# Half of the addition of four sum pairs a tile moved from VectorE to GpSimd, in a pairwise-interaction tower

## What is computed

```python
e = jnp.stack([tbl_0[ids[:, 0]], ..., tbl_31[ids[:, 31]]], axis=1)   # (1024, 32, 64)
p, q = e[:, ROW_IDX], e[:, COL_IDX]              # all pairs i < j: 496
z = jnp.einsum('bne,hne,bnh->bn', p, kernel, q)  # kernel (64, 496, 64)
h = jnp.concatenate([z, dense_ctx], axis=1)      # 496 + 16 = 512
h = jnp.maximum(h @ W_top1 + b_top1, 0.0)        # 512 -> 512
h = jnp.maximum(h @ W_top2 + b_top2, 0.0)        # 512 -> 256
y = h @ W_top3                                   # 256 -> 1
```

## Time and profile before

| | us |
|---|---|
| timed runs, median of 3 | 391.67 (391.31 to 391.91) |
| profiled execution, its span | 467.8 |
| TensorE matmuls busy | 402.3 |
| VectorE busy | 354.2 |
| ScalarE busy | 335.2 |
| GpSimd busy | 241.7 |

### The profile page before, as it was taken

One profiled execution on the slowest core, in us unless ns is written; L12 is line 12 of the kernel. 1 busy time (PEld: TensorE's weight loads), 2 busy tenths in 40 slices (PEclk: granted clock), 3 DMA queues, 4 the chain that ended last, 5 costly groups with the idle time before them and its releaser, 6 DMA issues.

```text
span 467.8 us, 13484 instructions
## 1 busy us (share of the span) xinstructions
PE 402.3 (86%) x4800; PEld 298.7 (64%) x4800; DVE 354.2 (76%) x449; ACT 335.2 (72%) x2889; POOL 241.7 (52%) x260
## 2 busy tenths in 40 slices
PE   0537869598898989999999989999999989999997
PEld 0425645467766776677756776677757776668765
DVE  0226757577888978887888978887887978888982
ACT  1216656658689685969689685969689685969894
POOL 5555555545555556555555555555555555552000
PEclk9978789799999999999999999999999999999999
DMA  3564560101111011101111011101111111110000
GB/s 73 180 207 158 165 190 18 21 18 22 22 24 22 19 24 22 23 22 22 21 26 21 20 24 22 23 20 22 22 23 24 20 24 22 22 21 15 2 2 1
DMA packets 14563, 19.27 MB, mean 41 GB/s; under 512 B 7192, under 2 KB 7840, under 8 KB 14496
## 3 DMA queue, kind: packets, MB, share of 16 engines
q0 software_dynamic: 8192, 8.40, 9.1%
q1 hardware_dynamic: 6304, 10.00, 6.7%
HBM read 18.39 MB, written 0.00 MB: 39 GB/s over the span
## 4 chain that ended last, share of the span: by engine, by line
PE 61%; DVE 18%; issue 9%; another core or an unknown queue 6%; ACT 3%; POOL 1%; DMA 1%; DVEq 0%
PE u_ps L628 24%; PE u_ps L621 20%; DVE prod_s L537 9%; PE side_ps L642 9%; DVE prod_t L520 6%; ACT prod_s L432 3%; PE side_ps L677 2%; PE u_ps L604 2%; PE acc_ps L677 2%; DVE h L551 2%; POOL emb L383 1%; PE u_ps L708 1%; PE side_ps L701 1%; DVE emb_t L509 1%
## 5 line engine op out<-in xcount | busy, mean ns | idle before, releaser
L432 ACT ACTIVATE prod_s<-prod_s 128x64 f32<-128x64 f32 x1405 | 307.9, 304 | 76.2 <-DVE prod_s L537 66.2
L383 POOL DMA_INDIRECT emb<-tbl,ids_sb x256 | 241.5, 943 | 184.5 <-issue 44.6
L432 ACT ACTIVATION_READ_ACCUMULATOR prod_s<-prod_s 128x1 f32 x1405 | 266.5, 230 | 3.6 <-issue 3.4
L520 DVE TENSOR_TENSOR prod_t<-u_ps,emb_t 128x1024 f32<-128x1024 f32 x128 | 154.1, 1219 | 54.7 <-remote 35.4
L621 PE MATMUL u_ps<-emb_t,k_sb 64*128 64x128 f32 x2048 | 159.1, 286 | 27.6 <-issue 13.9
L621 PEld LDWEIGHTS u_ps<-emb_t,k_sb 64*128 64x128 f32 x2048 | 146.2, 194 | 52.0 <-issue 29.6
L537 DVE TENSOR_TENSOR prod_s<-u_ps,emb 128x1024 f32<-128x1024 f32 (+4 forms) x224 | 150.8, 721 | 25.7 <-PE u_ps L628 11.7
L628 PE MATMUL u_ps<-k_sb,emb_t 64*128 64x512 f32 (+5 forms) x704 | 147.5, 503 | 15.1 <-DVE prod_s L537 10.5
L628 PEld LDWEIGHTS u_ps<-k_sb,emb_t 64*128 64x128 f32 x704 | 63.8, 196 | 51.8 <-issue 18.1
L642 PE MATMUL side_ps<-prod_t,pick_sb 128*32 128x256 f32 x1024 | 66.6, 387 | 0.1
L642 PEld LDWEIGHTS side_ps<-prod_t,pick_sb 128*32 128x32 f32 x1024 | 35.4, 111 | 21.4 <-issue 6.0
(11 more groups left out here) (27 smaller groups left out, 43.5 us busy)
## 6 DMA issues: line engine op xcount, KB each, us to landing
k_sb<-k_pairs SPq DMA_DIRECT2D x9, 512.0 KB, 4.5
emb<-tbl,ids_sb POOLq DMA_INDIRECT x256
k_sb<-k_pairs SPq DMA_DIRECT2D x6, 480.0 KB, 5.0
w_sb<-w SPq DMA_DIRECT2D x1, 1024.0 KB
w_sb<-w SPq DMA_DIRECT2D x1, 512.0 KB
k_sb<-k_pairs SPq DMA_DIRECT2D x1, 448.0 KB
h<-dense SPq DMA_DIRECT2D x8, 8.0 KB
out<-y_row SPq DMA_DIRECT2D x8, 0.5 KB
```

Source lines behind the costliest of these rows:

```text
L383: nc.gpsimd.indirect_dma_start(emb[t % EMBS][:, f * EMBED:(f + 1) * EMBED], None, tables[f], bass.IndirectOffsetOnAxis(ap=ids_sb[:, t, f:f ...
L432: done = nc.scalar.activation(slot, slot, ACT.Copy, accum_out=to[:, column:column + 1])
L520: done = nc.vector.tensor_tensor(prod_t[at % TRING][:].rearrange("p (h x) -> p h x", h=HALVES), u, low.unsqueeze(1).to_broadcast([P, HALVE ...
```

## The change

In seven tiles (all but tile 0) four of the eight sums of VectorE (k = 2, 6, 8, 10) are split. GpSimd adds, for each of the eight slots of the pair, the upper 32 columns to the lower 32, in place (`add_halves`), and VectorE sums 32 columns a slot. The add stands on GpSimd's queue behind the gather tied to block 10, 18, 24 or 28 (`HALVED_BEHIND`) and waits for the products' `slot_emptied`; VectorE's sum moves behind the multiply of block 14, 22, 28 or 31 (`HALVED_SUM_AT`) and waits for the new semaphore `halves_added`. `two_runs` moves out of VectorE's part unchanged.

```diff
--- before.py
+++ after.py
@@ -136,6 +136,29 @@
     ("u", 28), ("u", 29), ("u", 30), ("u", 31)]

 assert len(GATHER_AT) + len(OWN_GATHER_AT) == FIELDS and len(SECOND_GATHERS) == len(GATHER_AT)
+
+
+
+HALVED_BEHIND = {10: 2, 18: 6, 24: 8, 28: 10}
+HALVED_SUM_AT = {2: 14, 6: 22, 8: 28, 10: 31}
+HALVED = sorted(HALVED_SUM_AT)
+
+
+def halved(t, k):
+
+    return t > 0 and k in HALVED
+
+
+def halved_before(t, k):
+
+    return max(t - 1, 0) * len(HALVED) + sum(j < k for j in HALVED if t > 0)
+
+
+def gather_behind(n):
+
+    early = [f for f, (kind, at) in enumerate(GATHER_AT) if kind == "u" and at == n]
+    own = [f + len(GATHER_AT) for f, (kind, at) in enumerate(OWN_GATHER_AT) if kind == "u" and at == n]
+    return 1 if early else 0, (early + own)[0]


 def gather_step(t, f):
@@ -321,6 +344,7 @@
         slot_filled = sem("slot_filled")
         slot_emptied = sem("slot_emptied")
         summed_v = sem("summed_v")
+        halves_added = sem("halves_added")
         summed_a = sem("summed_a")
         acc_copied = sem("acc_copied")
         picked = sem("picked")
@@ -353,10 +377,34 @@
             at = (t * NS + S_INDEX[n]) % SRING
             return prod_s[:, at * HALVES * BANK:(at + 1) * HALVES * BANK]

+        def two_runs(start, step):
+
+            both = prod_s[:, start:start + 2 * step] if start + 2 * step <= SRING * HALVES * BANK else None
+            if both is None:
+                both = prod_s[:, start + ON_DVE * EMBED - step:start + ON_DVE * EMBED + step]
+                return both.rearrange("p (k x) -> p k x", k=2)[:, :, step - ON_DVE * EMBED:].rearrange(
+                    "p k (n e) -> p k n e", e=EMBED)
+            return both.rearrange("p (k x) -> p k x", k=2)[:, :, :ON_DVE * EMBED].rearrange(
+                "p k (n e) -> p k n e", e=EMBED)
+
+        def pair_products(t, k):
+
+            first, second = STRAIGHT_AT[k], STRAIGHT_AT[k + 1]
+            step = HALVES * BANK + (BLOCKS[second].slots - BLOCKS[first].slots) * EMBED
+            start = (t * NS + k) % SRING * HALVES * BANK + (SLOTS + BLOCKS[first].slots - ON_DVE) * EMBED
+            return two_runs(start, step)
+
         block = ctx.enter_context(nc.Block())

         @block.gpsimd
         def _(pool):
+            def add_halves(t, k):
+
+                pool.wait_ge(slot_emptied, used(t, STRAIGHT_AT[k + 1]))
+                products = pair_products(t, k)
+                low, high = products[:, :, :, :EMBED // 2], products[:, :, :, EMBED // 2:]
+                nc.gpsimd.tensor_tensor(low, low, high, ALU.add).then_inc(halves_added, 1)
+
             pool.wait_ge(first_ids_loaded, 16)
             for t in range(TILES):
                 if t == 1:
@@ -384,6 +432,13 @@
                         emb[t % EMBS][:, f * EMBED:(f + 1) * EMBED], None, tables[f],
                         bass.IndirectOffsetOnAxis(ap=ids_sb[:, t, f:f + 1], axis=0),
                     ).then_inc(arrived, 16)
+                    for n, k in HALVED_BEHIND.items():
+                        ahead, gather = gather_behind(n)
+                        if f == gather and t - ahead > 0:
+                            add_halves(t - ahead, k)
+            for n, k in HALVED_BEHIND.items():
+                if gather_behind(n)[0]:
+                    add_halves(last, k)

         @block.sync
         def _(sp):
@@ -545,21 +600,13 @@
                     upper = buffer(t, second)[:, BANK:BANK + (ON_ACT - LAST_SHARED) * EMBED]
                     nc.vector.tensor_reduce(h0[t % H0S][:, LAST_SHARED:ON_ACT],
                                             upper.rearrange("p (n e) -> p n e", e=EMBED), AX_X, ALU.add)
-                step = HALVES * BANK + (BLOCKS[second].slots - BLOCKS[first].slots) * EMBED
-                start = (t * NS + k) % SRING * HALVES * BANK + (SLOTS + BLOCKS[first].slots - ON_DVE) * EMBED
+                products = pair_products(t, k)
+                if halved(t, k):
+                    dve.wait_ge(halves_added, halved_before(t, k) + 1)
+                    products = products[:, :, :, :EMBED // 2]
                 column = ON_ACT + k * ON_DVE
                 nc.vector.tensor_reduce(h0[t % H0S][:, column:column + 2 * ON_DVE].rearrange("p (k n) -> p k n", k=2),
-                                        two_runs(start, step), AX_X, ALU.add).then_inc(summed_v, 1)
-
-            def two_runs(start, step):
-
-                both = prod_s[:, start:start + 2 * step] if start + 2 * step <= SRING * HALVES * BANK else None
-                if both is None:
-                    both = prod_s[:, start + ON_DVE * EMBED - step:start + ON_DVE * EMBED + step]
-                    return both.rearrange("p (k x) -> p k x", k=2)[:, :, step - ON_DVE * EMBED:].rearrange(
-                        "p k (n e) -> p k n e", e=EMBED)
-                return both.rearrange("p (k x) -> p k x", k=2)[:, :, :ON_DVE * EMBED].rearrange(
-                    "p k (n e) -> p k n e", e=EMBED)
+                                        products, AX_X, ALU.add).then_inc(summed_v, 1)

             for t in range(TILES):
                 for n in range(NB):
@@ -570,8 +617,11 @@
                         copy_turned(t, own_turns(t)[n])
                     if early_turn(t, n):
                         copy_turned(t + 1, 0)
-                    if n > 0 and not TURNED[n - 1] and S_INDEX[n - 1] % 2 == 1:
+                    if n > 0 and not TURNED[n - 1] and S_INDEX[n - 1] % 2 == 1 and not halved(t, S_INDEX[n - 1] - 1):
                         sum_two(t, S_INDEX[n - 1] - 1)
+                    for k in HALVED:
+                        if halved(t, k) and n == HALVED_SUM_AT[k]:
+                            sum_two(t, k)
                 if not TURNED[NB - 1]:
                     sum_two(t, NS - 2)
             dve.wait_ge(weights_loaded, 80)
```

## The result

| | median us | runs | lowest to highest |
|---|---|---|---|
| before | 391.50 | 8 | 390.77 to 392.29 |
| after | 392.93 | 8 | 391.71 to 394.25 |

The ratio is 1.0042 (95% interval 1.0029 to 1.0056): the change makes the kernel slower by 0.4%, about 1.6 us. That lies inside the predicted range, but the change went the other way than the forecast of 388.0. Of all timed runs in this document one, of 577.8 us at a granted clock of 0.58, was in a slow state, and it is left out of its kernel's median.

What follows compares the result with a forecast made beforehand. The prediction took VectorE to bound the timed runs: 391.67 - 7.5 (shorter sums) + 2.4 (GpSimd's adds) + 1.4 (code load) = 388.0 us. The range was 384.2 to 397.8, the forecast's own 386.6 to 389.7, chance 0.38.

Steps and rivals of the forecast that it cites:

- it must be VectorE: In the timed runs VectorE alone sets the pace, near 44.2 us a tile, so removed VectorE work saves its full length.
- The sum of VectorE's work and idle ends: VectorE's 354.2 us of work, 15.0 idle at the start and 8.3 at the end: 377.5 of 391.67 us.
- nothing changes: Rival, chance 0.15: TensorE or ScalarE is as near as VectorE, or the sums get no cheaper; 391.0 to 392.4 us.
- What I said would break the sum: VectorE's durations being shorter in timed runs than in the profile; then it isn't the bound, and time stays unchanged.
- The moved sums finish before their ring buffers are written again, so that adds no wait: On VectorE, sums at later places finish before their buffers are rewritten (blocks 5 and 6 by 22), costing no wait.
- my rivals for slower: GpSimd becomes the bound, 403.7 us (397.8 at 1.25 an add), chance 0.22; adds and VectorE block each other, 407.4, chance 0.08.
- The sums: On VectorE, 28 sums read 256 elements instead of 512, each 0.267 us shorter: 7.5 us less, 1.07 a tile.
- The new wait: On VectorE, the late sum's wait for GpSimd's add, costed at zero while GpSimd keeps up.
- The adds: On GpSimd, four adds a tile at 0.83 us each with handover, 3.3 us, bringing GpSimd to 43.3 us a tile.
- The 2.4 us: Time given back because GpSimd needs 0.4 us a tile more than VectorE's 42.9, over 5.9 tiles.
- The code load: An extra instruction before GpSimd's first add loads code, assumed 4.5 us; VectorE loses 1.4 us of it, once.
- The port: Rival, chance 0.08: GpSimd's adds and VectorE's operations hold each other up, 0.83 us an add, giving 407.4 us.

## Why the prediction was wrong

**The account.** Worked out from the table, the 0.33 us a tile that the change costs come out of two parts. From the whole sums moved: k = 8 and 10 add 1.13 us a tile, k = 2 adds 0.59 and k = 6 takes it back, so the places cost 1.13. Halving gives back 0.27 for each sum that stands where it counts: k = 2, 8 and 10 at their new places, 0.81; k = 6 at 22 is free and gives none. 1.13 - 0.81 = 0.32; measured +0.33.

**The bound.** The step that failed is "it must be VectorE", with the price drawn from it, "its full length, until another engine is in the way". The sum of VectorE's work and idle ends was right about its tile (44.0 to 44.2, and 43.96 was measured), but not about VectorE being alone: TensorE's stretches, passed back and forth through three PSUM slots, take just as long. That it came so near is in part luck: VectorE is busy 348.9 us on a faster chip and not 354.2, since its instructions, as long as before, overlap more where they follow each other without a wait; and tile 0 has 10.3 us of idle time behind VectorE's first instruction where I gave it about 14. Half sums at the old places are worth 0.33 us a tile and not 1.07, so 7.5 us should have been about 2.3. The rival "nothing changes" named the reason, TensorE as near, but 392.93 lies above its 391.0 to 392.4, since it didn't have the places.

**The profile.** I read 76 us between span and timed runs as an execution under the profiler that was slower, and expected the span after at 466 to 469. All points to another chip (no run names the chip of that profile): profiled span and timed time differ by about 2 us on either (468.2 and 469.3; 389.7 and 391.7). The page gave no view of the tile in which the times arose, where TensorE's matmuls fill 43.9 of 43.9 us. What I said would break the sum, shorter durations of VectorE in timed runs, did not occur (a whole sum takes 676 ns in the earlier trace rows and 676 in the profile after); 0.68 us of idle time a tile was left to VectorE.

**The places.** "The moved sums finish before their ring buffers are written again, so that adds no wait" looked at one constraint only. This is the second step that failed, and the one that turned the sign: it priced the move at nothing, and the move costs 1.13 us a tile. Tiles 1 to 7 together are 6.8 us longer with whole late sums, of 7.3 us in the timed runs. No rival had this mechanism: my rivals for slower were both on GpSimd, and the adds alone (1.0015) rule both out.

**The sums.** Right: 28 at 409 ns, 267 less each, 7.5 us less work.

**The new wait.** Right: zero. The adds of tile 3 end 3.4 to 4.8 us before their sums start.

**The adds.** 0.60 us with the handover, where I took 0.83 from the bounds 0.10 and 1.25. GpSimd then needs 32 x 1.25 + 4 x 0.60 = 42.4 us a tile and not 43.3, and nothing comes back. The 2.4 us were wrong, as the adds alone (1.0015, with 1 inside the interval) say too.

**The code load.** 0.11 us once for the 4.5 assumed, so 1.4 us too many. My reason, that a load has to come from memory, had no row behind it, and no row shows whether the extra instruction loads anything here. The Trainium skill's 6 us for the first call to a freshly loaded kernel (GPSIMD Engine Reference, Instruction dispatch) did not show here either.

**The port.** Right that it isn't one: VectorE's turned products of 1024 columns take 1213 ns with the adds alone, 1212 in the kernel before on the same chip. In the changed kernel 39 of the 128 run while an add does, and their mean is 1216 ns, as for the other 89. The Trainium skill's rule (SBUF — State Buffer, SBUF: two separate sides) agrees with that.

**Open.** Why one chip takes 52.6 us for a tile that the other does in 43.96, at the same granted clock. VectorE's and ScalarE's busy times in a tile are within 2% of each other on the two. What the traces show is the side it is on: in tile 3 of the slower chip TensorE's weight loads of the blocks idle 6.1 us for which the profile shows no releaser, where it is 1.8 on a faster one, and VectorE in turn waits. Tile 7, in which gathers are few, takes 47.4, so part of it may go with the gathers, but no run took them away. What late whole sums gain (0.25%) and the adds lose (0.34%) there isn't explained. Nor is it known what TensorE alone would need for a tile; 43.23 us were reached only with part of its work left out.

## What to carry to other kernels

When two engines hand slots to each other and both read nearly full, an instruction's price is set by where it stands: ahead of a wait it is free up to the length of that wait, elsewhere it costs its length, and moving it can cost or gain more than shortening it. List the waits of the engine within one period, with their lengths, and place the movable work just ahead of them; shorten only what stands elsewhere. A place where the other engine comes just in time is no such wait: work put there costs in full, and work taken away there gains nothing. And where a profiled span and the timed runs differ by a fifth, profile again before reasoning, since they may come from different chips.

## What the runs showed of the hardware

- The same program takes 391.7 us on one chip (391.2 to 391.7 on four) and 469.3 on another, with the granted clock at 1.00 in the tiles of both. VectorE's busy time in a tile is 43.22 and 43.89 us, TensorE's 43.90 and 49.01.
- An add on GpSimd of 256 columns in the 2x4x32 pattern takes 741 ns. It starts 0.95 us behind the start of the gather ahead, whose own 0.94 it follows at once, and the gather behind it starts 0.16 us behind its end; a gather behind a gather starts after 0.30. So among gathers it costs 0.60 us, less than its own length.
- GpSimd's first elementwise operation starts 1.06 us behind the start of the gather ahead, the others 0.95 to 0.97, so 0.11 us later once. Two instructions of 32 ns stand there on its queue's own row; what they bring isn't shown:

```profile
L406 POOLq MODIFY_POOL_CONFIG  x2: 32/32/32, 87.0 to 87.1; - x2
```
